# First token rows and conditioning vector issued from ScalarE's queue in an adaLN block with linear attention and experts

## What is computed

```python
mod = (_silu(c) @ wmod).reshape(2, 6, 1, -1)
sa, ca, ga, sb, cb, gb = (mod[:, 0], mod[:, 1], mod[:, 2], mod[:, 3], mod[:, 4], mod[:, 5])
ga = (2 * (ga >= 0) - 1) * jnp.maximum(jnp.abs(ga), 0.25)   # gb alike
h = _layernorm(x, axis=-1) * (1 + ca) + sa
x = x + ga * attention(h)
h = _layernorm(x, axis=-1) * (1 + cb) + sb
x = x + gb * experts(h)
```

## Time and profile before

| | before |
|---|---|
| median of 3 runs | 445.36 us (444.96, 445.36, 451.19) |
| the profiled execution | 446.77 us |
| its span, first to last instruction | 445.0 us |
| PE busy | 395.6 us (89%) |
| DVE, ACT, POOL busy | 239.5, 144.7, 145.4 us |
| DMA moved | 38.77 MB, mean 87 GB/s |

### The profile page before, as it was taken

How to read it: one execution, slowest core, us unless ns; L and a number is a source line. 1 busy time by engine, 2 the same in 40 slices (tenths; PEclk the granted TensorE clock), 3 DMA queues, 4 the chain that set the end, 5 groups by cost and what they waited for, 6 DMA issues and landing times.

```text
span 445.0 us, 9784 instructions
## 1 busy us (share of the span) xinstructions
PE 395.6 (89%) x3829; PEld 241.8 (54%) x3830; DVE 239.5 (54%) x559; ACT 144.7 (33%) x295; POOL 145.4 (33%) x250
## 2 busy tenths in 40 slices
PE   2987989999899998987999998729999999999784
PEld 2445566476658566435646644414466666666353
DVE  3168666899697787212553731003245655565367
ACT  2466618444761602440213111000243343333000
POOL 8304104300610430020000077754026676667400
PEclk9999999999999999997999999956999999999898
DMA  8999100000000000492000023332033333321097
GB/s 265 281 301 265 28 4 1 3 3 4 1 3 3 1 4 3 141 283 63 0 0 1 1 85 109 110 102 80 6 92 95 111 108 98 104 78 48 33 329 237
DMA packets 32269, 38.77 MB, mean 87 GB/s; under 512 B 4191, under 2 KB 29154, under 8 KB 32228
## 3 DMA queue, kind: packets, MB, share of 16 engines
q1 hardware_dynamic: 28820, 29.68, 23.2%
q0 software_dynamic: 3408, 8.51, 5.4%
HBM read 22.19 MB, written 16.90 MB: 88 GB/s over the span
## 4 chain that ended last, share of the span: by engine, by line
PE 69%; DVE 13%; issue 7%; ACT 4%; DMA 4%; SPq 1%; POOL 0%; DVEq 0%; POOLq 0%; ACTq 0%
PE work L1320 13%; PE at_ps L1661 11%; PE work L1330 7%; PE work L1349 4%; PE work L1682 4%; PE work L1684 3%; PE at_ps L1384 2%; PE work L1521 2%; PE work L1471 2%; PE at_ps L1349 2%; DMA arena<-ys_tokens 2%; PE at_ps L1645 2%; DVE arena L1086 2%; DMA hs<-in_wmod 1%; PE at_ps L1521 1%
## 5 line engine op out<-in xcount | busy, mean ns | idle before, releaser
L1330 PE MATMUL work<-sdn_sb,hs 128*128 128x256 f32 x192 | 51.0, 405 | 16.6 <-issue 13.7
L602 POOL DMA_INDIRECT ys_tokens<-er_pos,goal_u x39 | 40.9, 1049 | 46.2 <-DVE er_pos L1243 39.0
L573 POOL DMA_INDIRECT xs_sorted<-h2tok,pos_u x32 | 31.5, 986 | 73.2 <-DVE pos_u L934 63.7
L1661 PE MATMUL at_ps<-arena 128*128 x156 | 54.5, 472 | 0.4 <-ACT arena L826 0.4
L1330 PEld LDWEIGHTS work<-sdn_sb,hs 128*128 128x128 f32 x192 | 34.7, 193 | 33.0 <-issue 25.4
L1008 DVE TENSOR_TENSOR hs<-work,hs 128x512 f32<-128x512 f32 (+1 forms) x24 | 16.6, 692 | 64.0 <-PE work L1320 47.8
L622 ACT ACTIVATE hs<-work 128x512 f32<-128x512 f32 (+1 forms) x24 | 14.3, 596 | 104.6 <-PE work L1320 87.5
L536 POOL TENSOR_TENSOR sq<-sq,sg 128x512 f32<-128x512 f32 x8 | 10.0, 1271 | 103.6 <-issue 103.6
L1320 PE MATMUL work<-h2T,sup_sb 128*128 128x512 f32 x80 | 37.8, 621 | 0.6 <-DVE hs L1008 0.3
L1661 PEld LDWEIGHTS at_ps<-arena 128*128 128x128 f32 x156 | 26.5, 190 | 14.9 <-issue 6.6
L830 ACT ACTIVATE arena<-at_ps 128x176 f32<-128x176 f32 x39 | 12.4, 317 | 57.7 <-PE at_ps L1661 43.0
(11 more groups left out here) (243 smaller groups left out, 766.8 us busy)
## 6 DMA issues: line engine op xcount, KB each, us to landing
xs_sorted<-arena SPq DMA_DIRECT2D x10, 526.0 KB, 12.1
h2tok<-xs_sorted SPq DMA_DIRECT2D x20, 263.0 KB
arena<-ys_tokens SPq DMA_DIRECT2D x8, 512.0 KB, 7.3
arena<-in_e_up SPq DMA_DIRECT2D x8, 352.0 KB, 5.5
x_sb<-in_x SPq DMA_DIRECT2D x4, 512.0 KB, 7.3
out_rows<-x_sb SPq DMA_DIRECT2D x16, 128.0 KB, 4.9
sup_sb<-in_s_up SPq DMA_DIRECT2D x2, 640.0 KB, 5.0
hs<-in_wmod SPq DMA_DIRECT2D x1, 1024.0 KB, 8.2
```

Source lines behind the costliest of these rows:

```text
L573: g.indirect_dma_start(out=xs_dram, out_offset=bass.IndirectOffsetOnAxis(ap=pos_u[:, k, t:t + 1], axis=0), in_=h2tok[:, t, :], in_offset=N ...
L602: g.indirect_dma_start(out=ys_dram, out_offset=bass.IndirectOffsetOnAxis(ap=goal_u[:, i:i + 1], axis=0), in_=yout[:, q % 2, u, :], in_offs ...
L1330: ins = t_.matmul(o[:, t * HID:(t + 1) * HID], hs[0:m, f, tk], sdn_sb[0:m, f, :], start=(f == 0), stop=(f == FTS - 1))
L1661: ins = t_.matmul(at_ps[2 + u % 2][:, 0:2 * FE], xT[:, u % 2, k * P:(k + 1) * P], eup[:, bass.ds(e, 1), k, :].rearrange("p a n -> p (a n)" ...
```

## The change

The two loads that stood first in SP's program, the first token rows and the conditioning vector, are taken out of it, and ACT issues them as its first two instructions, before it waits for the vector. The modulation weights are now the first in SP's queue. Nothing else is changed; later lines of the file move up by two until the new place.

```diff
         @block.sync
         def _(sp):
-            sp.dma_start(x_sb[:, 0:TPB, :], x[0:BLK, :].rearrange("(t p) c -> p t c", p=P)).then_inc(ld_x[0], 16)
-            sp.dma_start(csb[:, :, :], cT).then_inc(ld_c, 16)
             sp.dma_start(wmod_sb[:, :, 0:2 * HID], wmod.rearrange("(k p) n -> p k n", p=P)[:, :, 0:2 * HID]
                          ).then_inc(ld_mod, 16)
@@
         def _(act):
             a = nc.scalar
             steps = Steps(act, act_step)
+            act.dma_start(x_sb[:, 0:TPB, :], x[0:BLK, :].rearrange("(t p) c -> p t c", p=P)).then_inc(ld_x[0], 16)
+            act.dma_start(csb[:, :, :], cT).then_inc(ld_c, 16)
             act.wait_ge(ld_c, 16)
             a.activation(csil[:, :, :], csb[:, :, :], ACT.Silu).then_inc(csil_ready, 1)
```

## The result

| | before | changed |
|---|---|---|
| median of 19 runs each, on one chip | 446.35 us | 450.30 us |
| lowest, highest | 443.97, 451.19 | 447.28, 453.27 |
| ratio, 95% interval | | 1.0103 (1.0076 to 1.0129) |
| profiled execution, span | 446.77, 445.0 us | 448.67, 446.9 us |

The ratio, 4.6 us of 446.35, compares the runs in the chip's faster state alone, and so differs a little from the 3.95 us between the medians. The forecast was a loss of 1.5 us, with a range that ended at 448.9. The sign was right, the size was not. About 1 us of the distance from the forecast 446.9 to 450.30 us is the median of before, which is 446.35 us over 19 runs and was 445.36 over three.

What follows compares the result with a forecast made beforehand. PE, busy 395.6 of 445.0 us, was taken to bound the kernel, so its start counts in full. Issue 0, ACT 0 and start of PE +1.5 us on the 445.36 us median gave 446.9 us, range 443.9 to 448.9.

Steps and rivals of the forecast that it cites:

- a loss of 1.5 us: Start of PE's line 1480: 12.9 us instead of 11.41, so the median goes from 445.36 to 446.9 us.
- Issue and ACT's own cost: Start of SyncE and ACT: weights issued 1.04 us earlier, ACT's two DMAs hidden before the vector lands; both counted 0.
- Packet by packet: DMA engines at the start take one packet from each queue in turn; 446.9 us, chance 0.42.
- The third rival: Long turns: engines take 16 packets from one queue at a time; vector may land about 8.6 us; 446.5 us, chance 0.15.
- Rows at 8.55 us: First token rows' landing: second half goes beside the second weights' 4 KB packets, so they land at 8.55 us.
- The vector 0.13 us behind the rows: Conditioning vector's landing: queued behind the rows, 0.13 us after them as before, at 8.7 us.
- xn is whole 4.28 us later: DVE's xn before line 1480: whole 4.28 us after the rows land, as before, at 12.83 us.
- The sign that the forecast named for a start after 13.5 us: Line 1480 starting later than 13.5 us would mean the queues hinder each other beyond their bytes.
- the clock case: Rival: moved start leaves PE at 1.2 GHz for 12 us more busy time, costing 6 us; 452.9 us, chance 0.06.

Runs made afterwards that it cites:

- Experiment 1: Changed kernel, but POOL waits for xn before its two long memsets; ratio to the kernel before 1.0051 (1.0007 to 1.0094).

## Why the prediction was wrong

- **Issue and ACT's own cost** were right: ACT's two DMAs took 0.52 and 0.52 us (0.45 and 0.49 were assumed), and the first table load ended at 3.2 us, hidden.
- **Packet by packet** was right for the stretches in which both queues had packets under way, 128 to 130 and 93 to 90, and wrong for the others, 101 to 10 and 52 to 375. The Trainium skill (DMA: Bandwidth & Descriptors, section Queues, rings and completion order) has turns of some 9 to 17 descriptors. With the vector's 8 packets per engine such a turn would have let them through at once; here they ran one beside each 4 KB packet for about 2 us (45 of 47 from 6.9 to 7.4 us). The measurement decides. The third rival falls with it, although its 8.6 us for the vector came near the 8.93 measured.
- **Rows at 8.55 us**: 7.1 was measured. I let the second half of the rows go beside 4 KB packets; for the most part they went ahead of them. From 5 to 6.25 us ACT's queue moved 375 packets to SyncE's 52. The step was too dear by 1.4 us.
- **The vector 0.13 us behind the rows** is the first step that failed. I carried a distance over from a queue without company, against my own packet rule: 8 small packets per engine, each behind a packet of 172 ns, are by estimate 1.4 us. Measured were 1.8 us. With it ACT's second table load (1.28 us) and rstd, which the forecast had put at nothing, came onto the path: xn began at 11.24 us, 4.1 after the rows, where 2.8 had been assumed. The two errors nearly cancel: xn would have been whole at about 12.7 us, and 12.83 was forecast.
- **"xn is whole 4.28 us later"** is the step that failed and decided. It was taken from a profile in which xn is written before POOL's long memsets begin. I noted that xn had 2.76 us of slack, but never asked what the time after 9.46 us held for DVE. POOL's memsets there are on no chain of before, and they stop DVE: 3.8 us of the 4.96. Experiment 1 removes just that and leaves 1.1 us. The sign that the forecast named for a start after 13.5 us, queues that hinder each other beyond their bytes, would have pointed the wrong way.
- The Trainium skill has the mechanism (SBUF — State Buffer, section Who interferes with whom): DVE and GpSimd share a port pair, DVE's copy and tensor_scalar can need it, and whoever is first has it for the whole instruction. The trace agrees, with 3.74 us for a tile of 0.40 us. It goes further: the tile that met the end of one memset also waited for all of the next.
- **Chances and range**: the clock case (0.06) was not what happened; the granted clock was even a little higher in the profile after (0.969 against 0.958). The range ended at 448.9 us since no mechanism in it reached past 2 us at the start. Within 2% was right.

## What to carry to other kernels

When a change moves an instruction later, take its duration from the company that it will have and not from the one it had: look in the timelines of all engines at what runs in the stretch into which it slips, here POOL's long memsets beside DVE's 0.4 us tiles. Of two queues with work, the load of small packets can lose most, since it may pay one large foreign packet for each of its own: the vector's 2 KB came 4.4 us later than before, the rows' 512 KB 2.75. Try a tiny load that gates a chain at the head of a queue, and look at what is issued beside it in the same moment. A swap of two lines in one queue brought PE's start from 11.41 to 10.05 us, where the second queue brought it to 16.37; at the end its ratio of 0.9959 is just at the edge of the noise.

## What the runs showed of the hardware that I had not expected

- Two queues that both have packets under way alternate one for one, whatever their sizes (128 to 130, 93 to 90). But a head start of 0.49 us gives the first load nearly all of the engines, rows at 4.3 us instead of 7.1, and from 5 to 6.25 us one queue moved 375 packets to the other's 52.
- A DVE instruction that meets a POOL memset can wait for those behind it too: a tile of 0.40 us took 5.75 us, begun 0.16 us after the first of three memsets (1.84, 3.55 and 0.56 us) and ended 0.15 us after the last.
- 2 KB of small packets between two large loads made the second land 1.35 us later, 7.72 against 6.37 us, while a third load stood directly behind; with that one held back it was 6.60 us.
